# Decoder layer on one core: epsilon and negated mean of the layer norms go to GpSimd, two kinds of one-value copies go, and all six queues get a new order

## What is computed

```
x = _layernorm(x + attn(x))          # a: scan "attention": causal conv, cos/sin features, weighted running sums
x = _layernorm(x + xattn(x, ctx))    # b: autocorrelation attention: FFT products, top-5 lags, softmax, sum of shifted values
x = _layernorm(x + ffn(x))           # c: 2 x 8 experts, product with running sums, softmax router
def _layernorm(x, axis=-1, eps=1e-05):
    m = jnp.mean(x, axis=axis, keepdims=True)
    v = jnp.var(x, axis=axis, keepdims=True)
    return (x - m) / jnp.sqrt(v + eps)
```

## Time and profile before

| | us |
|---|---|
| median of 3 runs (lowest, highest) | 893.53 (892.78, 893.91) |
| the profiled execution: its time | 892.9 |
| its span in the trace | 891.1 |
| what lies around the span | 1.8 |

### The profile page before, as it was taken

How to read it: one execution, slowest core, us unless ns; L and a number is a source line. 1 busy time by engine, 2 the same in 40 slices (tenths; PEclk the granted TensorE clock), 3 DMA queues, 4 the chain that set the end, 5 groups by cost and what they waited for, 6 DMA issues and landing times.

```text
span 891.1 us, 11684 instructions
## 1 busy us (share of the span) xinstructions
PE 823.9 (92%) x4040; PEld 489.4 (55%) x4040; DVE 754.2 (85%) x1351; ACT 488.0 (55%) x774; POOL 98.0 (11%) x164
## 2 busy tenths in 40 slices
PE   6886738999999999999999999999999999997996
PEld 3343515564755566565666475555656475656453
DVE  7987998899989998899989999899999996384133
ACT  4964763774558553866377545955395655202300
POOL 2021012000120012001120012001200022001000
PEclk9998968999999999999999999999999999999899
DMA  9475035232634343153622562234515251410040
GB/s 299 126 141 118 0 72 119 72 83 48 131 59 137 86 86 61 25 142 71 118 64 68 130 119 53 55 83 95 107 26 128 59 109 23 95 24 1 1 118 24
DMA packets 45968, 75.18 MB, mean 84 GB/s; under 512 B 4819, under 2 KB 28630, under 8 KB 45910
## 3 DMA queue, kind: packets, MB, share of 16 engines
q1 hardware_dynamic: 38998, 49.27, 22.3%
q0 software_dynamic: 6912, 25.17, 14.4%
HBM read 19.90 MB, written 4.19 MB: 27 GB/s over the span
## 4 chain that ended last, share of the span: by engine, by line
PE 48%; DVE 30%; DMA 8%; issue 8%; ACT 4%; SPq 1%; POOL 1%; ACTq 0%; DVEq 0%; POOLq 0%
DVE sc L2528 7%; PE ps L902 7%; DMA acc<-sq 7%; PE ps L911 7%; PE ps L867 6%; PE ps L785 5%; DVE sc L2520 4%; PE ps L709 4%; PE ps L751 3%; PE ps L927 3%; PE ps L726 3%; PE ps L769 2%; DVE zc L2458 2%; PE ps L844 2%; DVE frac L2500 2%
## 5 line engine op out<-in xcount | busy, mean ns | idle before, releaser
L2528 DVE TENSOR_TENSOR_SCAN sc<-mask,sc 128x1024 f32<-128x1024 bf16 x64 | 144.3, 2276 | 0.1
L911 PE MATMUL ps<-x2t,mv 128*128 128x512 f32 x256 | 119.0, 597 | 0.2
L902 PE MATMUL ps<-cum,mw 128*128 128x512 f32 x256 | 117.8, 596 | 0.6 <-DVE prod L2748 0.5
L927 PE MATMUL ps<-up,prod 128*128 128x256 f32 x512 | 115.3, 382 | 0.1
L927 PEld LDWEIGHTS ps<-up,prod 128*128 128x128 f32 x512 | 96.0, 190 | 17.6 <-issue 5.2
L2271 POOL DMA_DIRECT2D acc<-sq x48 | 42.3, 923 | 504.3 <-ACT sq L1570 491.5
L1570 ACT ACTIVATE sq<-sc 128x1024 f32<-128x1024 f32 x48 | 50.0, 1051 | 63.3 <-DVE sc L2528 45.0
L911 PEld LDWEIGHTS ps<-x2t,mv 128*128 128x128 f32 x256 | 47.4, 190 | 57.7 <-issue 51.1
L2520 DVE TENSOR_TENSOR sc<-sc,g 128x1024 f32<-128x1024 f32 x64 | 76.4, 1212 | 3.2 <-ACT sc L1554 3.0
L902 PEld LDWEIGHTS ps<-cum,mw 128*128 128x128 f32 x256 | 47.1, 190 | 55.0 <-issue 48.7
L2458 DVE SCALAR_TENSOR_TENSOR zc<-ps,cst,zc 128x510 f32<-128x510 f32 (+2 forms) x96 | 70.7, 744 | 6.6 <-ACT zc L1484 4.3
(11 more groups left out here) (226 smaller groups left out, 1357.5 us busy)
## 6 DMA issues: line engine op xcount, KB each, us to landing
acc<-sq POOLq DMA_DIRECT2D x48, 512.0 KB, 4.5
wb<-wT SPq DMA_DIRECT2D x64, 256.0 KB, 3.7
xt<-in_x_t_dram SPq DMA_DIRECT2D x8, 512.0 KB, 5.7
cin<-in_ctx_dram SPq DMA_DIRECT2D x8, 512.0 KB, 5.3
frac<-den SPq DMA_DIRECT2D x32, 128.0 KB, 3.7
xs_a<-in_x_dram SPq DMA_DIRECT2D x8, 512.0 KB, 5.5
out_dram<-prod SPq DMA_DIRECT2D x16, 256.0 KB, 4.0
per<-zs SPq DMA_DIRECT2D x32, 64.0 KB
```

What stands on the lines that cost most here:

```text
L902: last = mm(o, mw[:, t, br, c:c + P], cum[:, t, :], start=(t == 0), stop=(t == 1))
L911: last = mm(o, mv[:, t, br, c:c + P], x2t[:, t, :], start=(t == 0), stop=(t == 1))
L927: return mm(o, prod[:, j, q * P:(q + 1) * P], up[:, j, :], start=(j == 0 and q % 2 == 0), stop=stop)
L2528: V.tensor_tensor_scan(flat, mask[:, 0:2 * T], flat, 0.0, ALU.mult, ALU.add)\
```

## The change

Four edits:
- `layer_norm`: the copy to `seen`, the wait behind `bn_aggr` and the two small VectorE operations (epsilon, negated mean) are left out. `rstd` on GpSimd now waits for the second `bn_aggr` of the half and does both itself, with constant tiles `eps_` and `minus` that VectorE fills once at the start.
- `b_topk`: the copy of one value ahead of the max of eight is left out.
- The lists of steps that the semaphores count by are adapted: `eps neg` move from VectorE's lists to GpSimd's.
- All six lists of steps are written in another order (same steps on each engine).

```diff
-LAYER_NORM = each("res", range(2)) + each("stats aggr", range(NQ)) + each("eps neg", range(2))
+LAYER_NORM = each("res", range(2)) + each("stats aggr", range(NQ))
-POOL_A = Steps("pool_a", each("rstd shift", range(2)))
+POOL_A = Steps("pool_a", each("eps neg rstd shift", range(2)))
-        half_ = sb("half_", [P, NQ])
+        half_, eps_, minus = (sb(n, [P, NQ]) for n in ("half_", "eps_", "minus"))
...
-                pool.wait_ge(*VEC.at(i, "eps", n))
+                pool.wait_ge(*VEC.at(i, "aggr", 2 * n + 1))
+                G.tensor_tensor(rs[k][:, 2, q], mvr[k][:, q, 1], eps_[:, q], ALU.add).then_inc(*OWN.tick("eps", n))
+                G.tensor_tensor(rs[k][:, 3, q], mvr[k][:, q, 0], minus[:, q], ALU.mult).then_inc(*OWN.tick("neg", n))
+                pool.wait_ge(*OWN.at(i, "eps", n))
                 G.tensor_tensor(rs[k][:, 0, q], rs[k][:, 2, q], half_[:, q], ALU.pow).then_inc(*OWN.tick("rstd", n))
+                pool.wait_ge(*OWN.at(i, "neg", n))
                 pool.wait_ge(*OWN.at(i, "rstd", n))
-                pool.wait_ge(*VEC.at(i, "neg", n))
                 G.tensor_tensor(rs[k][:, 1, q], rs[k][:, 3, q], rs[k][:, 0, q], ALU.mult).then_inc(*OWN.tick("shift", n))
...
+            V.memset(eps_[:, :], EPS)
+            V.memset(minus[:, :], -1.0)
...
                 dve.wait_ge(*VEC.at(i, "stats", 2 * n + 1))
-                V.tensor_copy(seen[:, k:k + 1], st[k][:, 2 * n, 0:1])
                 for r in range(2 * n, 2 * n + 2):
                     V.bn_aggr(mvr[k][:, r, :], st[k][:, r, :]).then_inc(*VEC.tick("aggr", r))
-                dve.wait_ge(*VEC.at(i, "aggr", 2 * n + 1))
-                TS(rs[k][:, 2, q], mvr[k][:, q, 1], EPS, None, ALU.add).then_inc(*VEC.tick("eps", n))
-                TS(rs[k][:, 3, q], mvr[k][:, q, 0], -1.0, None, ALU.mult).then_inc(*VEC.tick("neg", n))
...
                 dve.wait_ge(*VEC_B.at(i, "corr"))
-                V.tensor_copy(sm[:, 12:13], cor[:, 0, 0:1])
                 V.max(top, c).then_inc(*VEC_B.tick("top"))
```

More of the change, by code:

```diff
@@ L118 @@
 ACT_B = Steps("act_b", each("xf cf", range(2)) + ["ot"] + SPEC + ["exp", "wt"] + NORM)
-POOL_B = Steps("pool_b", each("rstd shift", range(2)))
+POOL_B = Steps("pool_b", each("eps neg rstd shift", range(2)))
 VEC_B = Steps("vec_b", each("fold", range(4)) + each("ot", range(2)) + each("pr", range(3)) + ["heads", "ca", "cb0", "cb1", "cb2", "corr", "top", "negmax",
@@ L128 @@
 ACT_C = Steps("act_c", each("xT", range(2)) + each("h", range(4)) + ["logit", "exp", "wT"] + NORM)
-POOL_C = Steps("pool_c", each("rstd shift", range(2)))
+POOL_C = Steps("pool_c", each("eps neg rstd shift", range(2)))
 VEC_C = Steps("vec_c", ["cum", "max", "sub", "sum", "inv", "weight", "copies"]
@@ L507, in _ @@
             load_residual(4)
+            store(1, 0)
+            store(1, 1)
+            spread(2, 5)
             spread(2, 6)
@@ L572, in _ @@
             spread(7, 0)
+            spread(7, 2)
             spread(7, 1)
-            spread(7, 2)
-            spread(7, 6)
[L576 to L580, removed]
+            spread(7, 4)
+            spread(7, 5)
+            spread(7, 3)
+            spread(7, 7)
+            store(6, 0)
+            spread(7, 6)
             store(6, 1)
@@ L978, in _ @@
             fold(16)
+            a_sums(0, 1)
             fold(17)
@@ L987, in _ @@
             fold(25)
+            a_squares(0)
+            a_project(1, 0)
             a_sums(0, 2)
             a_sums(0, 3)
[L990 to L993, removed]
             a_scores(1)
@@ L1173, in _ @@
             b_wt(3)
-            a_sums(4, 1)
             b_wf(3)
@@ L1217, in _ @@
             a_sums(5, 0)
-            a_sums(5, 1)
+            c_own(3, 2)
             c_own(3, 3)
@@ L1288, in _ @@
             a_squares(6)
+            a_sums(6, 2)
             b_back(5)
-            a_sums(6, 2)
             a_sums(6, 3)
+            a_project(7, 0)
             b_out(5, 0)
             b_out(5, 1)
-            a_project(7, 0)
             a_out(6, 0)
@@ L1686, in _ @@
             a_project(0, 2)
+            a_exp(0)
             a_turns(0, 0)
             a_linear(0, 0)
+            fold(0)
+            a_turns(0, 1)
+            a_project(0, 3)
             a_linear(0, 1)
-            a_project(0, 3)
-            fold(0)
             fold(1)
@@ L1788, in _ @@
             b_wt(0)
+            a_squares(1, 4)
             a_squares(1, 5)
+            a_gate(1, 1)
+            a_guard(1)
             a_squares(1, 6)
@@ L1796, in _ @@
             b_layer(0, 1)
+            a_scores(2)
+            c_transpose(0, 0)
+            c_transpose(0, 1)
+            c_hidden(0, 0)
             a_project(2, 0)
@@ L1929, in _ @@
             c_transpose(2, 1)
+            a_project(4, 0)
+            a_layer(3, 0)
+            a_layer(3, 1)
             a_project(4, 1)
@@ L2793, in _ @@
             a_scan(0, 7)
+            a_den(0)
             biases()
@@ L2802, in _ @@
             a_residual(0, 0)
+            a_den(1)
             a_residual(0, 1)
@@ L2970, in _ @@
+            b_topk(2)
+            c_prod(1, 5)
+            a_moments(3, 4)
+            b_weight(2)
+            c_scale(1, 6)
+            a_moments(3, 5)
+            c_prod(1, 6)
+            c_scale(1, 7)
+            c_prod(1, 7)
+            a_scan(3, 4)
+            a_scan(3, 5)
             a_moments(3, 6)
-            a_scan(3, 5)
             a_moments(3, 7)
```

1107 lines of the change are left out of this document (542 added, 565 removed).

## The result

| | before | after |
|---|---|---|
| median of 5 runs (lowest, highest), us | 893.65 (892.78, 896.20) | 906.24 (904.29, 908.45) |
| ratio, 95% interval | 1 | 1.0138 [1.0117, 1.0158] |
| profiled execution, us | 892.9 | 908.45 |
| its span, us | 891.1 | 906.3 |
| `c_transpose(0)` begins | 156.19 | 161.75 |

The changed kernel is 1.4% slower, where 0.2% faster was forecast. The two rows on `c_transpose` split the 15.2 us by which the spans differ (the profiled execution after is the slowest of the five): +5.6 until `c_transpose(0)`, +9.5 from there to `c_transpose(7)`, +0.1 behind it. DVE does 13 us less, and the kernel is slower all the same. Not all of the loss is waiting.

The account below looks back on a forecast made before the run. PE was taken as the bound from 160 to 800 us, with DVE (91% busy) close behind. Start -0.5, middle -0.9 and tail -0.7 sum to -2.1: 890.8 profiled, 891.4 us as median; range 886.5 to 898.0.

Parts of the forecast that it names:

- DVE per half: Each half of a norm on DVE: without copy, epsilon and mean the next step starts 0.33 us earlier.
- GpSimd per half: Each half of a norm on GpSimd: from aggregation to power 0.50 us instead of 0.28, with two added operations.
- GpSimd becomes late: Rival: GpSimd's added operations are held, PE loses 0.9 us at c_transpose in each of 8 chunks, 898.6 us; chance 0.14.
- The two constant tiles are filled at the start while DVE waits for the constants: nothing: At the start on DVE: filling the two new constant tiles was claimed to cost nothing.
- The middle, -0.9 within 6.5 either way: From 160 to 800 us: one long PE wait for a residual gained, -0.9 us, bounds -6.5 and +6.5.
- the prediction's sign of being wrong: In the middle: PE's idle time over 8 us would show the forecast wrong.
- The start, -0.5: Until c_transpose(0): four terms, -1.13 + 1.1 + 0.3 - 0.75, summing to -0.5 us.
- the late scores: At the start: a_exp(0) behind three projections makes the six spreads late for DVE, 1.1 us, bounds 0 and 4.4.
- the late sums: At the start: a_sums(0, 2) and (0, 3) behind a_squares(0) and a_project(1, 0), 0.3 us, bounds 0 and 3.5.
- The tail, -0.7: Last chunk and end: -0.5 us from an earlier last aggregation less GpSimd's delay, -0.2 us at the very end.
- The rival with a stalled queue: Rival: in the new order spread(0, 3) stands behind spread(0, 5) and so c_prod(0, 1), DVE waits, 898.0 us; chance 0.12.
- The end of the range, 898.0: Upper edge of the range over all cases, 886.5 to 898.0 us; the ends of the two slow cases lie there.

Follow-up runs that it names:

- copies_only: The kernel before with only the one-value copies taken away, old order, epsilon and mean still on DVE: 892.76 us, ratio 0.9990.
- gp_late: The kernel before with epsilon and mean on GpSimd, copies kept, old order, the two constant tiles declared behind all others: 892.83 us, ratio 0.9990.
- edits_late: The changed kernel with the old order of steps and the two constant tiles declared behind all others: 891.79 us, ratio 0.9977 to before.
- after_late: The changed kernel, new order kept, with the two constant tiles declared behind all others: 900.94 us, ratio 1.0080 to before.
- after_fix: after_late with a_squares of chunks 2 to 7 one or two steps later on PE: 900.65 us, ratio 1.0092 to before.
- after_scan: after_late with unit 4's scan directly behind its a_moments and unit 2's add ahead of unit 3's, in most chunks: 905.60 us, ratio 1.0132 to before.
- edits_scan4: edits_late with unit 4's scan moved directly ahead of unit 5's in chunks 2, 3, 5, 6, 7, squares and some adds following: 902.92 us, 1.0104 to before.

## Why the prediction was wrong, step by step

**DVE per half: right.** 0.33 us freed was forecast. Where DVE goes straight on, it takes 0.53 from the end of the statistics to its next step before and 0.20 after (22 of the halves); the copy's share is 0.06 (copies_only, 0.47). The Trainium skill's section on the DRAIN (VectorE: DVE Perf Modes) would have made it 0.48; the trace disagrees here as it did in the earlier trace rows.

**GpSimd per half: right, a little better.** 0.50 from aggregation to power was forecast, 0.38 is the measured median; where the first operation is held, up to 0.74 and in two halves over 2. The rival "GpSimd becomes late" (0.14) is out: gp_late is at 0.9990. Its sign, slower, came true for another reason.

**"The two constant tiles are filled at the start while DVE waits for the constants: nothing".** This step failed. I priced filling them, not where they lie. Their place costs 0.5 to 0.6%, some 5 us, more than twice what the edits win.

**The middle, -0.9 within 6.5 either way.** This is the step that failed most. I let hundreds of moves cancel, "for which no row speaks more than for the other". A row did: the wait at `a_squares` was among PE's longest in the middle before, 1.4 us in two waits, a chain of DMAs with little slack; and the order lines of the diff (these are not among the ones printed above) took the scan of unit 4 in chunks 2, 3, 5 and 7 from its own place to one behind the expert products, just ahead of that of unit 5. The middle lost 9.5 us in the profiled execution, over the bound of 6.5, 7.1 of it idle time of PE; the prediction's sign of being wrong, over 8 of idle time there, came with 14.7. That the adds' chain carries most of this is shown by the runs without the last adds; which of the moves made it late is shown for none by itself. The bound was wrong too: a late chain adds idle time that was not there, so the idle time of before limits only the gain.

**The start, -0.5.** It was +5.6. The terms I had were fair: 1.1 for the late scores was 0.26, 0.3 for the late sums 0.21. Two moves were not in the sum. `b_fold(0, xf)` went behind `a_conv(1, 2)` and a fraction, which is 2.9 us between the first `a_poly` of chunk 1 and it (95.66 - 88.56 after, 90.58 - 86.37 before). And `a_squares(0)` waited 3.50 instead of 1.66. Rows of before:

```profile
65.65 0.64 PE L739 MATMUL ps<-acc,cst 128*32 128x256 f32 x8 [1.66 <-DMA acc<-sq]
...
90.58 0.68 DVE L2586 TENSOR_TENSOR xs_a<-x 128x512 f32<-128x512 f32 x1
```

Neither is shown to carry the loss. With the tiles as before, `c_transpose(0)` begins at 156.25 in the old order (edits_late), and in the new one at 159.30, 158.30 and 156.82 (after_late, after_fix and after_scan, whose steps until then differ in one pair of adds at most): 0.6 to 3.1 later, although `b_fold(0, xf)` is as late in all three (93.94 to 94.96, against 90.67 in edits_late). The sum also had no term for the clock: 3.1 of the 5.6 is PE busy for longer at a granted clock of 0.86 instead of 0.89. Whether the new waits brought that down no run separates.

**The tail, -0.7.** Small and partly right: PE's wait ahead of the last `c_transpose` is 4.38, from 4.55, where 4.0 was forecast: 0.17 of 0.5.

**What was right by a sum that fits.** The edits without the new order and with the tiles out of the way, edits_late, take 891.79, and 891.4 was forecast for the whole, new order included: that they meet is chance. The shares within it are not shown to be those of my sum. The rival with a stalled queue (0.12) named the right kind, a transfer late through the new order, but the wrong queue: the spreads of SP instead of the adds of GpSimd. The end of the range, 898.0, was its price for one stall (the 898.6 of the GpSimd rival lay just outside); the chain stalls in every chunk.

## What to carry to other kernels

A new tile, even of 16 bytes, is part of the layout: declare small ones behind the large tiles, or pad them to 256 bytes, and compare the DMA queues' shares of the span before and after, since packets and bytes show nothing. When a new order is judged, look for the longest chain that alternates engines and DMAs through a single buffer, count how many of its links are left when the consumer comes, and price every move of a link at up to a full landing (4.5 us here; the five moves of edits_scan4 cost 2.2 each), not at nothing. Time freed on an engine that is 91% busy can be worth little: 13 us less on DVE gave 2.

## What the runs showed of the hardware

That the start address of tiles, within 256 bytes, changes the time of SBUF-to-SBUF adding DMAs (4.5 to 4.6 or 4.7 us a transfer of 512 KB, 128.3 to 133.6 us of the queue) I had not expected to see in the kernel's time at all. The second is that the hold of GpSimd's operations fell on whichever came first in the half: with two short operations ahead of it the power's mean over the three norms fell from 0.86 to 0.70 us, and the first added operation of the a norm had a mean of 0.35, the one behind it 0.19 (both rows of POOL's groups):

```profile
L2245 POOL TENSOR_TENSOR rsa<-mvra,eps_ 128x2 f32<-128x2 f32 x16 | 5.6, 353 | 57.6 <-DVE mvra L2564 57.6
...
L2246 POOL TENSOR_TENSOR rsa<-mvra,minus 128x2 f32<-128x2 f32 x16 | 3.1, 194 | 0.0
```
